# Opening each stage from the one before it, and another order in narrow attention, in a fused two-layer transformer kernel

## The reference, cut

```python
def _L0_xattn_ref(x, context, ...):
    x = _attn(_ln(x, g1, b1), _ln(x, g1, b1), Wq1, Wk1, Wv1, Wo1, bo1) + x    # 16 heads of 64
    x = _attn(_ln(x, g2, b2), context, Wq2, Wk2, Wv2, Wo2, bo2) + x           # 16 heads of 64
    x = _geglu_ff(_ln(x, g3, b3), Wp, bp, Wf, bf) + x
    return x

def _L1_xattn_ref(x, xf, ...):                                                # 16 heads of 16
    q, k, v = x @ Wq + bq, xf @ Wk + bk, xf @ Wv + bv        # cut in heads
    probs = softmax(q * SCALE @ k.T)
    out = probs @ v @ Wo + bo
    h = gelu(((out - mu) * rsqrt(var + LN_EPS) * ln_g + ln_b) @ W1 + b1)
    out = out + h @ W2 + b2
    return x + out
```

## Time and profile before

| | us |
|---|---|
| three runs | 1557.21, 1556.76, 1553.67 (median 1556.76) |
| the profiled execution | 1555.33 |
| its span (first to last instruction) | 1553.6 |
| TensorE busy | 1425.3 (92%), mean granted clock 0.967 |
| VectorE, ScalarE, GpSimd busy | 965.5 (62%), 873.3 (56%), 371.8 (24%) |

### The profile page before, as it was taken

How to read it: one execution, slowest core, us unless ns; L and a number is a source line. 1 busy time by engine, 2 the same in 40 slices (tenths; PEclk the granted TensorE clock), 3 DMA queues, 4 the chain that set the end, 5 groups by cost and what they waited for, 6 DMA issues and landing times. The chain is left out here.

```text
span 1553.6 us, 30742 instructions
## 1 busy us (share of the span) xinstructions
PE 1425.3 (92%) x12194; PEld 1206.3 (78%) x12194; DVE 965.5 (62%) x1768; ACT 873.3 (56%) x2431; POOL 371.8 (24%) x537
## 2 busy tenths in 40 slices
PE   5999999989999999999999969996989899897697
PEld 4787878768888888888888858995777677775586
DVE  5556474658767776777677754545666756665442
ACT  3455473755555665665566544332767667576454
POOL 2010110042211221112111000004565646462100
PEclk9999999989999999999999969997999999999799
DMA  9000000002000000000000002001000000000000
GB/s 246 9 1 1 1 1 1 1 28 97 9 9 8 14 11 9 9 9 8 9 8 9 1 1 83 1 1 28 14 16 17 17 9 17 16 9 1 1 24 24
DMA packets 25070, 30.30 MB, mean 20 GB/s; under 512 B 1408, under 2 KB 22880, under 8 KB 24672
## 3 DMA queue, kind: packets, MB, share of 16 engines
q1 hardware_dynamic: 24928, 28.33, 6.4%
HBM read 26.49 MB, written 1.84 MB: 18 GB/s over the span
## 5 line engine op out<-in xcount | busy, mean ns | idle before, releaser
L832 ACT ACTIVATE B_probs<-banks,B_neg_max 112x375 f32<-112x375 f32 x256 | 143.5, 574 | 111.3 <-DVE B_neg_max L932 111.3
L1627 ACT ACTIVATE D_probs<-banks,D_neg_max 112x375 f32<-112x375 f32 x256 | 143.5, 573 | 62.7 <-DVE D_neg_max L1722 62.7
L1722 DVE TENSOR_REDUCE D_neg_max<-banks 112x2 f32<-112x750 f32 x128 | 114.1, 933 | 92.9 <-PE banks L1849 92.9
L780 POOL TENSOR_TENSOR B_q_hi<-B_q_group,ones 128x224 fp32r<-128x224 f32 x64 | 36.8, 575 | 407.9 <-PE banks L1041 360.5
L932 DVE TENSOR_REDUCE B_neg_max<-banks 112x2 f32<-112x750 f32 x128 | 114.2, 934 | 28.0 <-PE banks L1041 26.9
L633 PE MATMUL banks<-B_ctxT,B_wk_hi 128*128 128x378 f32 x384 | 115.7, 355 | 1.6 <-issue 1.5
L633 PE MATMUL banks<-B_wv_hi,B_ctxT 128*126 128x512 f32 x288 | 105.9, 421 | 0.0
L1856 PE MATMUL banks<-ident,D_probs 112*126 112x112 f32 x780 | 101.4, 267 | 4.2 <-DVE D_probsT L1727 4.1
L940 DVE TENSOR_SCALAR B_probs<-B_probs,B_rsums 112x375 f32<-112x375 f32 x256 | 102.0, 441 | 4.5
L949 DVE TENSOR_TENSOR B_k_lo<-banks,B_k_hi 128x378 fp32r<-128x378 f32 x128 | 69.9, 548 | 53.0 <-ACT B_k_hi L846 53.0
L1064 PE MATMUL banks<-ident,B_probs 112*126 112x112 f32 x768 | 95.8, 260 | 5.6 <-DVE B_probs L940 4.2
(11 more groups left out here) (332 smaller groups left out, 3931.7 us busy)
## 6 DMA issues: line engine op xcount, KB each, us to landing
ctx<-in_ctx_dram SPq DMA_DIRECT2D x32, 189.0 KB
ctx<-in_ctx_dram SPq DMA_DIRECT2D x32, 92.2 KB
w_stage<-in_L_xattn_Wq_dram SPq DMA_DIRECT2D x2, 1024.0 KB, 7.7
w_stage<-in_L_xattn_Wp_dram SPq DMA_DIRECT2D x1, 2048.0 KB, 8.2
w_stage<-in_L_xattn_W_dram SPq DMA_DIRECT2D x2, 1024.0 KB, 6.3
out_dram<-x_tokens SPq DMA_DIRECT2D x4, 448.0 KB, 3.2
x_tokens<-in_x_dram SPq DMA_DIRECT2D x1, 1344.0 KB, 19.3
w_stage<-in_L_xattn_Wk_dram SPq DMA_DIRECT2D x1, 1024.0 KB, 9.7
```

The lines of the kernel that those rows point to most:

```text
L832: nc.scalar.activation(P[:, c, 0:S], SB[0:N, c, 0:S], ACT.Exp, bias=nm[:, c:c + 1], accum_out=sm[:, c:c + 1]).then_inc(exp_done, 1)
L1627: nc.scalar.activation(P[:, m % 2, j, 0:S], SB[0:N, j, 0:S], ACT.Exp, bias=nm[:, m % 2, j:j + 1], accum_out=sm[:, odd, 4 * m + j:4 * m + j ...
L1722: nc.vector.tensor_reduce(nm[:, m % 2, 2 * half:2 * half + 2], SB[0:N, 2 * half:2 * half + 2, 0:S], AX.X, ALU.max, negate=True).then_inc(m ...
```

## The change

**Openings.** The statistics, power and normalisation of a stage's first group move to the last group of the stage before: A does them for B, B for C, C the plain copies for D, D statistics and normalisations (of `k.y`) for E. They write one shared tile (`k.xh`, ln_out) in place of one a stage; the semaphores of the next stage are counted up at its start (`first_is_ready`, `first_rstd_is_ready`), and SyncE waits at a stage's end for the normalisations. In B, ScalarE's copy and rounding of the first tokens come behind the rounding of Wk, no more behind that of Wq. In C and E, `act_full` of the first group comes ahead of a weight part.

**Pretended rows.** The steps of a row before the first go, on all engines, with the memsets that filled their tiles (five on GpSimd in A; in D those of P, PT, v, OB and the sums, of which the padding columns of P stay). The semaphores that they counted are counted up instead. `k.x` and `k.y` have no padded rows any more.

**C and E, in groups.** All four normalisations of the next group come at part j = 2, the transposes at 3 (from 4), `act_full` at 4 (from 5); the rounding stays at 5.

**D.** The four transposes of the sums come in one set behind the scores of m = 0, into the bank of the projection, and wait for the multiply; ScalarE evacuates them all ahead of its exponentials, and VectorE's evacuation goes. The keys of the first product wait for that evacuation. GpSimd's context split waits for the multiply; its x update comes at m = 2; its token splits come in two steps instead of four. In rows b = 3 the second transposes come ahead of the product.

The diff, cut:

```diff
+    k.xh = sb("ln_out", [N, GB, D])
...
+    def first_is_ready(self, dve):
+
+        for s in (self.stats_done, self.mean_done, self.norm_done):
+            dve.sem_inc(s, GB)
+
+    def first_rstd_is_ready(self, pool):
+        pool.sem_inc(self.var_done, 1)
+        pool.sem_inc(self.rstd_done, 1)
...
-            nc.gpsimd.memset(k.x[:, 1 + B:1 + B + GB, :], 0.0).then_inc(k.pad_set, 1)
-            nc.gpsimd.memset(k.x[:, 0, :], 0.0).then_inc(k.pad_set, 1)
-            nc.gpsimd.memset(P[:, 1, :, :, :].rearrange("p j u n -> p (j u n)"), 0.0).then_inc(init, 1)
-            nc.gpsimd.memset(PT[:, :, :, :].rearrange("p j u n -> p (j u n)"), 0.0).then_inc(init, 1)
-            nc.gpsimd.memset(v[:, GB - 1, :], 0.0).then_inc(init, 1)
...
             for g in range(NG):
+                ln.pool_rstd(nc, pool, k, g + 1)
                 if g < NG - 1:
-                    ln.pool_rstd(nc, pool, k, g + 1)
                     ln.split(nc.gpsimd, k, g + 1)
...
-                    if u == 0:
+                    if u == 0 and g:
                         o_evac(g * STEPS, 0)
...
-                    if s in (1, 2) and g < NG - 1:
+                    if s == 1 and g == NG - 1:
+                        dve.wait_ge(x_done, X0 + 1 + GB)
+                    if s in (1, 2):
                         ln.dve_stats(nc, dve, g + 1, 2 * s - 2)
...
-                    if s in (3, 4) and g < NG - 1:
+                    if s in (3, 4):
...
             def tail(i, t, n):
+                if i == 0:
+                    return
...
-            pe.wait_ge(init, 4)
+            pe.sem_inc(av_done, 2)
+            pe.sem_inc(t_done, 2)
+            pe.sem_inc(y_done, 1)
...
-                if i == 1:
+                if i == 0:
...
-            for b in range(GB):
-                ln.dve_stats(nc, dve, 0, b)
-            ln.dve_mean(nc, dve, 0, True)
+            dve.sem_inc(o_lo, 1)
+            dve.sem_inc(y_out, 1)
...
-                        if not last:
-                            if b == 0:
-                                ln.dve_stats(nc, dve, g + 1, m)
-                                if m == 3:
-                                    ln.dve_mean(nc, dve, g + 1)
-                            if b == 1 and m < 2:
-                                ln.dve_norm(nc, dve, g + 1, 2 * m)
-                                ln.dve_norm(nc, dve, g + 1, 2 * m + 1)
+                        if last and b == 0 and m == 0:
+                            dve.wait_ge(x_done, X0 + 1 + GB)
+                        if b == 0:
+                            ln.dve_stats(nc, dve, g + 1, m)
+                            if m == 3:
+                                ln.dve_mean(nc, dve, g + 1)
+                        if b == 1 and m < 2:
+                            ln.dve_norm(nc, dve, g + 1, 2 * m)
+                            ln.dve_norm(nc, dve, g + 1, 2 * m + 1)
...
-                        values(i - 1, (m - 1) % 4)
+                        if i:
+                            values(i - 1, (m - 1) % 4)
...
-                            if t == 0:
+                            if t == 1:
                                 pe.wait_ge(wo_lo, 1)
-                            project(0)
+                            if t:
...
+                if i == 0:
+                    ln.act_full(nc, act, 0, TB)
                 if i == (1 if gated else 0):
-                    ln.act_full(nc, act, 0, TB)
                     ln.act_round(nc, act, 0)
...
+                    if j == HT // 2 and g < NG - 1:
+                        ln.act_full(nc, act, g + 1, TB)
                     if j == HT // 2 + 1 and g < NG - 1:
...
+                    if g == NG - 1 and gated and j == 2:
+                        dve.wait_ge(x_done, 2)
+                        for b in range(GB):
+                            ln.dve_norm(nc, dve, NG, b, norm=False)
...
-                    if j in (2, 3):
-                        for b in range(2 * j - 4, 2 * j - 2):
+                    if j == 2:
+                        for b in range(GB):
...
-                    if j == HT // 2 and g < NG - 1:
+                    if j == HT // 2 - 1 and g < NG - 1:
...
-            nc.gpsimd.memset(k.y[:, 1 + B:1 + B + GB, :], 0.0).then_inc(k.ypad_set, 1)
-            nc.gpsimd.memset(P[:, :, :, :], 0.0).then_inc(init, 1)
-            nc.gpsimd.memset(PT[:, :, :, :].rearrange("p q j n -> p (q j) n"), 0.0).then_inc(init, 1)
-            nc.gpsimd.memset(v[:, 1, :, :, 0, :].rearrange("p s h d -> p (s h) d"), 0.0).then_inc(init, 1)
+            nc.gpsimd.memset(P[:, :, :, S:SP].rearrange("p q j n -> p (q j) n"), 0.0).then_inc(init, 1)
...
+                            pool.wait_ge(rce_done, t + 1)
...
-                        if m == 3:
-                            x_update(t)
-                        if g < NG - 1 and b == 2 and m < KT:
+                        if m == 2 and t > 1:
+                            x_update(t - 1)
+                        if g < NG - 1 and b == 2 and m == 1:
                             pool.wait_ge(l_out, GB * (g + 1))
-                            nc.gpsimd.tensor_tensor(ln.hi[:, m, :], ln.yf[:, m, :], k.ones[:, :].to_broadcast([128, GT]),
-                                                    ALU.mult).then_inc(ln.hi_done, 1)
-                        if g < NG - 1 and b == 2 and m >= KT:
-                            pool.wait_ge(ln.hi_done, (g + 1) * KT + m - KT + 1)
-                            nc.gpsimd.tensor_tensor(ln.lo[:, m - KT, :], ln.yf[:, m - KT, :], f32(ln.hi[:, m - KT, :]),
-                                                    ALU.subtract).then_inc(ln.lo_done, 1)
+                            for c in range(KT):
+                                nc.gpsimd.tensor_tensor(ln.hi[:, c, :], ln.yf[:, c, :], k.ones[:, :].to_broadcast([128, GT]),
...
-                act.wait_ge(rb_mm, 2 * t + 2)
-                nc.scalar.activation(rbs[:, 2 * N:4 * N].rearrange("p (j n) -> p j n", j=2), TB[:, :, SPARE:SPARE + N],
-                                     ACT.Copy).then_inc(rb_act, 1)
+                act.wait_ge(rb_mm, t + 1)
+                act.wait_ge(o_out, t)
+                nc.scalar.activation(rbs[:, :], PJ[:, 0:MT * N], ACT.Copy).then_inc(rb_act, 1)
...
-            for b in range(GB):
-                ln.dve_norm(nc, dve, 0, b, True)
...
-            def rsums_out(t):
-                dve.wait_ge(rb_mm, 2 * t + 1)
-                nc.vector.tensor_copy(rbs[:, 0:2 * N].rearrange("p (j n) -> p j n", j=2), TB[:, :, SPARE:SPARE + N]
-                                      ).then_inc(rb_dve, 1)
...
+                        if g == NG - 1 and b == 0:
+                            if m == 0:
+                                dve.wait_ge(y_out, Y0 + 1 + GB)
+                            ln.dve_stats(nc, dve, 0, m, k.y)
+                            if m == 3:
+                                ln.dve_mean(nc, dve, 0, True)
+                        if g == NG - 1 and b == 1:
+                            ln.dve_norm(nc, dve, NG, m, src=k.y, norm=True, rstd=1)
...
-            def rsums(half):
-                for j in range(2):
-                    m = 2 * half + j
-                    ins = nc.tensor.transpose(TB[:, j, SPARE:SPARE + N],
+            def rsums(t):
+                pe.wait_ge(rce_done, t + 1)
+                pe.wait_ge(y_out, t + Y0)
+                if t % GB == 0 and t < B:
+                    pe.wait_ge(q_act, t + 2)
+                for m in range(MT):
+                    ins = nc.tensor.transpose(PJ[:, m * N:(m + 1) * N],
                                               rce[:, 4 * m:4 * m + 4, :].rearrange("p j r -> p (j r)"), k.ident[0:N, 0:N])
                 ins.then_inc(rb_mm, 1)
 
...
-            turn(3, 0)
...
+                    pe.wait_ge(rb_act, t + 1)
...
-                    pe.wait_ge(rce_done, t + 1)
-                    rsums(0)
-                if m == 1:
-                    pe.wait_ge(rb_act, t + 1)
...
+                        if m == 0 and t:
+                            rsums(t)
...
-                        pe.wait_ge(pt_act, max(i, 1))
-                        values(odd if m >= 2 else 1 - odd, (m - 2) % 4, m % 2)
+                        if i > 1:
+                            pe.wait_ge(pt_act, i)
+                            values(odd if m >= 2 else 1 - odd, (m - 2) % 4, m % 2)
                         if b == 3:
+                            second_turn(g, b, t, m)
                             product(g, b, t, m, odd)
...
-                        if m == 0:
-                            pe.wait_ge(rb_dve, t + 1)
-                            rsums(1)
-                        else:
```

## The result

The changed kernel takes 1509.17 us (median of 4 runs, 1508.51 to 1509.67), the kernel before 1555.8 beside it; the ratio is 0.9701, 95% interval 0.9684 to 0.9718. The profiled execution took 1509.67 with a span of 1507.9, 45.7 less than the span of 1553.6.

The account below looks back on a forecast made before the run. TensorE was taken to bound cross attention, with idle time to win in narrow attention and stage openings. Gains 6.5 + 1.2 + 11.9 + 27.5 = 47.1 us; 1555.3 - 47.1 + 1.4 = 1509.6, said as 1509, range 1496 to 1524.

Parts of the forecast that it names:

- the 27.0 forecast: Self attention's opening: the seventh product starts at about 27.0 where it started at 33.18, with A_wo coming last; 6.2 us.
- the 2 taken off: Self attention: 2 us deducted since TensorE stands some 2 us before A_wo lands and may then run at half speed.
- The sign named for this stage: Self attention: no memset beside a normalisation, where four normalisations had taken 5.22 us beside GpSimd's memsets.
- the 0.5 put down: Cross attention's opening: 0.5 us gained, since moving 2.4 us of token rounding ahead of Wq delays Wq as much.
- All four terms: Feed forward stages: openings 2.8 (first) and 4.6 (last), waits inside groups 1.5 and 3.0; sum 11.9 us.
- 0.55 gained in each of 9 rows: Narrow attention, ordinary first steps: next scores 4.68 us after the first instead of 5.23; with three rows at 0.3, 5.8.
- 5.1 a row: Narrow attention, fourth rows of three groups: GpSimd's wait for the multiply removes 2.62 us of waiting and about 2.5 of clock.
- 1.45 a row: Narrow attention, fourth rows: cost of the other order, queries waiting for VectorE's evacuation in three steps; net gain 3.65 each.
- Half speed at new places: Rival 2: idle replacing pretended steps and longer query waits bring half speed at six places; +13, 1523 us; chance 0.14.
- the third rival: Last group of narrow attention: moved normalisations blocked in four places of 4.07 us, 1 of clock; +20, 1530; chance 0.04.
- the fourth rival: Narrow attention: multiply blocked by GpSimd's work in all 15 rows, 99 us on top, about 1608, slower than before; chance 0.03.
- TensorE in narrow attention under 92% busy: Narrow attention: a sign that the forecast is wrong; TensorE was busy 318 of 357.5 us before the change.

## Why the prediction was right, and where it was not

**Self attention: too small by 3.5.** The mechanism was right, A_wo comes last, at 13.29 + 12.7 = 25.99 for the 26.95 of before. The seventh product started at 26.03 for the 27.0 forecast, and the steps behind it gave 2.9 for 2.5. The term that failed is the 2 taken off: TensorE was to stand 2 us and fall to half speed. It stood 0.43, because six products that start at 16.48 end near 25.6, and the products behind it took 0.37 as those just ahead did. (The views have the granted clock at 1.00 from the span's start on; but the first ten products start 0.37 apart and the later ones 0.20, so that up to 19.9 the column doesn't fit.) The sign named for this stage came: the four normalisations take 1.61 without the memsets, for 5.22.

**Cross attention: right size, incomplete reason.** The first scores come 1.0 earlier after the stage's start, for the 0.5 put down; but in runs with the same code this differs by up to 1.0. The value step and the first half projection turned into waiting, as said. The second half projection did count at first, 12.3 between the third scores of both kernels where it was 11.1, and was lost again at the context load 7 us later, which the prediction did not look at. The load was 0.2 late before; with some 1.3 less ahead of it, it is 1.7.

**Feed forward stages.** All four terms were within 0.4, and the split over two parts is shown by its undoing, transposes and copies together.

**Narrow attention's ordinary rows: 3.1 for 5.8, and by another cause.** The step that failed is "0.55 gained in each of 9 rows", set down to the single set of transposes. The runs show that 0.28 to 0.48 of a first step is the multiply no longer beside the update, and that the single set adds nothing there in second and third rows: with the update put back, the single set has 5.27 for the 5.23 of the kernel before. The prediction had read this overlap in the earlier trace rows, 0.97 against 0.69, and took 0.69 into its chain, but set the gain down to the wait between the halves; VectorE's own chain (multiply, maxima, evacuations) is what TensorE waited for. And it left out what the last stage's opening costs in the last group: in row 13 statistics (0.42) and means (0.38) stand ahead of the multiply on VectorE, TensorE waits 0.95, and the step is 0.3 longer than before.

**Fourth rows: right size, wrong instruction.** The gain of the block and the clock was put at 5.1 a row; with the old order it is 5.2 (6.20 for 11.39), with the new one 4.7. It was credited to GpSimd's new wait. The step that failed is this one: that wait does nothing here. The moved x update ends the block, and the regrouped token splits alone leave only 0.5 of it. The prediction named the update only as an overlap that "moves", and said that only it overlaps; in the fourth rows a token split follows it without a gap and leads into the context split. The price of the new order was put at 1.45 a row; the three later steps cost 1.6, and the first 0.5 more, which was not in the sum: 2.1.

**Rivals.** Half speed at new places did not come: D's clock is 0.99, and the longest new wait behind the scores is 0.95. The moved normalisations of the third rival took 0.65, 0.41, 0.40 and 0.41: at most 0.25 more than the shortest, not 4.07. The blocked multiply of the fourth rival did not come (0.69 in 16 places); the kernel with GpSimd's old order shows what it costs in the new one: the first step of a fourth row takes 12.3 to 14.7, more than in the kernel before, because TensorE now stands at the transposes right behind the scores. That the errors, 3.5 too little in self attention and 4.5 too much in narrow attention, nearly cancelled is luck. "TensorE in narrow attention under 92% busy" was a bad sign to name: it is 90% in a kernel that gained 23 us there.

The Trainium skill (SBUF — State Buffer, Who interferes with whom) says that a VectorE instruction with two SBUF inputs contends with a GpSimd one that reads SBUF, and that the loser blocks for the whole instruction. The runs agree (0.97 to 1.18 beside one GpSimd instruction), and add that a row of GpSimd instructions without a gap counts as one (4.74 beside five).

## What to carry to other kernels

When one write releases an engine and its writer goes on with work on a resource that both share, look at everything that is queued behind the released instruction: it was one update, released just ahead of the multiply, that made a step nearly six microseconds longer three times, and moving it alone gave 19 us. Undo each part of a change that wins as a whole; here the reordering in the fourth rows cost 7 us that the changed kernel could have had. And a step taken off ahead of a load only pays if the load is early: after such a change, read the waits on DMAs again.

## What the runs showed of the hardware

- The multiply's length follows the GpSimd instructions that run when it starts: 0.69 with none, 0.97 to 1.18 with one update, 2.25 with an update and a token split followed by a pause of 0.63, 4.74 with an update, a token split and three parts of the context split. It ended 0.55 us after the last of them each time, and a pause of 0.15 was enough to let it in.
- After waits of 1.79 us behind the scores, three times with the same instructions, the granted clock fell to 0.50 twice and not at all once; the step took 10.97, 9.79 and 8.25.
- A load of 280 KB issued 3 us behind 3 MB took 9.6 us to be there (342.79 to 352.40), and was not late any more when issued ahead of them.
- In the last stage's opening TensorE starts at half clock, and how long it stays differs between executions of the same code. The granted clock of 2 us stretches, from 6 us after the stage's start on: in the changed kernel it is full from 8 us on, in the one without GpSimd's wait still 0.50 up to 10 us. The length of the stage does not follow it: 103.3 us in the first, 103.1 in the second.

```profile
1410.50:1412.50 2.00, 2.00 (x7) 1.75 (x6) 1.43 (x2) 1.98 (x2) 0.00 (x0) 0.51 0.00 0
1412.50:1414.50 2.00, 1.12 (x6) 0.69 (x4) 1.74 (x2) 1.96 (x4) 0.00 (x0) 1.00 0.00 0
```

```profile
1413.60:1415.60 2.00, 2.00 (x7) 1.57 (x5) 1.79 (x1) 1.96 (x3) 0.00 (x0) 0.50 0.00 0
1415.60:1417.60 2.00, 1.53 (x7) 1.13 (x7) 1.62 (x4) 1.24 (x3) 0.00 (x0) 0.83 0.00 0
```
